# Split start-up constants, a warmed array, clearing in pieces and single last tiles in a two-layer mixture-of-experts block on one Trainium2 core

## The chip, the cores and the metric

The kernel runs on one core of one Trainium2 chip. The metric is the device time in microseconds (us) of one execution. A second number, the span, is what the hardware profiler records from the first to the last instruction of one execution. Engines are named as in the profile: PE (matrix engine, with PEld for its weight loads), DVE (vector), ACT (scalar), POOL (GpSimd), SP (sync, which here only issues transfers). A "q" behind a name is that engine's instruction sequencer, which also issues transfers.

## The reference, cut to what matters

```
x: 8 x 512 tokens of 128 values
x = x + 0.5 * moe(layernorm(x))
x = x + attention(layernorm(x))        # 16 heads of 8, rotary positions
x = x + 0.5 * moe(layernorm(x))

def moe(x):                            # 4096 tokens, 16 experts, 256 places each
    gate = softmax(x @ Wg); idx = argmax(gate)
    loc  = number of earlier tokens with the same expert
    rows with loc < 256 go to expert idx, place loc
    h = relu(rows @ w1[idx]); y = h @ w2[idx]
    return y * gate[idx]  (0 for tokens with loc >= 256)
```

## The kernel before

**Stages.** Each engine has one program written out by hand; they meet only in semaphores. There are four stages in time. (1) Routing of layer 0: all 4,096 tokens are loaded as four groups of 8 tiles of 128 tokens, and a table is built that says for each expert place which token stands there. (2) The 16 experts of layer 0. (3) Attention over 8 sequences, with the second layer's routing spread over it. (4) The 16 experts of layer 1, which write the output.

**Stage 1.** SP issues the 8 loads of the tokens (`load_x`, two to a group), then four of `w1`. ACT issues six small loads, `routing_constants` (identity matrix, gate weights, counting matrices, two expert numberings, token numbers), all on one semaphore `consts_loaded`. PE and DVE both begin by waiting for all six. PE then averages the gate weights over the features (`average_gate`), turns the groups (`turn_group`, 8 transposes each), multiplies them with the centred gate (`group_logits`), counts (`count_group`) and adds to the table (`add_to_table`). ACT copies each turned group out of PSUM (`keep_group`) and behind each copy issues one 1 MB load of `w2` (`load_w2`); after the fourth it computes its share of the marks (`mark_last_places`, one call for each group), without which `add_to_table` can't go. DVE finds each token's expert (`choose_group`), its place (`place_group`), marks, and at the end reads the table (`read_table`, `token_of`). PE issues its steps in this fixed order, so `count_group` of group 2 stands behind `add_to_table` of group 0.

**Clearing.** A scratch tensor `slots` in DRAM (4,096 rows of 146 values) is filled by layer 1's routing and has to hold "no token" rows before that. ACT clears it with one 2.3 MB transfer behind its last mark, just ahead of the experts (`clear_slots`). POOL waits for it (`slots_cleared`) only after the 16 experts of layer 0.

**Experts.** For expert n of layer 0 POOL issues two indirect transfers (`gather_slots`, L725; 128 token rows each) that bring the 256 rows. DVE measures and centres them (L757, L774), PE turns them (`turn_slots`, L834), ACT copies (L870), PE multiplies with `w1` (L842), ACT rectifies (L874), PE multiplies with `w2` (L862: two tiles of 128 places, 8 instructions each), and DVE scales or adds (L786 in layer 0, L826 in layer 1). PE's order is: experts n+1 in, expert n out, with the turning of expert n+2 between the two tiles. `w1`, rows and results stand in rings of four, hidden values in rings of two. In layer 1 both output tiles are signalled by one increment, added by two DVE instructions with one increment (`y_used`), and written by two indirect transfers on POOL (`scatter_rows`, L886). POOL also computes a power of each expert's variance (`invert_slot_deviation`, L769), three experts ahead of the scatter:

```
for n in range(first, last):
    if n + 3 < last:
        invert_slot_deviation(pool, n + 3, (n + 3) % UNROLL)
    scatter_rows(pool, n)
```

ACT's exponentials of expert 31 (`slot_exponentials`) need that power.

**Filling.** `keep_array_busy(count, bank)` issues constant bf16 matmuls of 256 columns (L348); 48 stand between the table and the experts of layer 0.

## Time and profile before

| | |
|---|---|
| time, median of 3 runs | 613.0 us (612.53 to 613.96) |
| the profiled execution: its own time | 612.57 us |
| its span | 610.5 us |
| busy: PE, DVE, ACT, POOL | 561.8, 439.5, 374.0, 395.9 us |
| stage 1, to the end of `token_of` | 0 to 32.7 us |
| layer 0's experts, first turning to last output tile | 42.8 to 108.1 us |
| attention | to about 518 us |
| layer 1's experts, first turning to last scatter | 536.5 to 601.9 us |

The span is 2.1 us shorter than the execution's own time. Engine programs run side by side, so the busy sums say little about one stage; a stage is read from which instruction starts late in it, and from what that one waited for. In a row of the timeline, the text in brackets is the idle time ahead of the instruction and what ended it; "issue" there means that the profile shows no other engine or transfer as the releaser.

### The profile page before, as it was taken

How to read it: one execution, taken by the hardware profiler on the slowest of the kernel's cores; microseconds unless marked ns; L12 is line 12 of the kernel's file. 1: busy time of each engine (PE TensorE's matmuls, PEld its weight loads, DVE VectorE, ACT ScalarE, POOL GpSimd, SP SyncE). 2: the span in 40 equal slices, each digit the busy share in tenths (PEclk: the TensorE clock that was granted, in tenths of full speed). 3: DMA queues.
4: the chain of work that ended last, by engine and by line, in shares of the span. 5: the costliest groups of instructions: out<-in, count | busy, mean ns of one | idle time of the engine just before them, and what ended most of it. 6: DMA issues, size and time to landing. Idle time of an engine off the chain costs nothing.

```text
span 610.5 us, 13303 instructions
## 1 busy us (share of the span) xinstructions
PE 561.8 (92%) x4980; PEld 302.1 (49%) x4980; DVE 439.5 (72%) x938; ACT 374.0 (61%) x518; POOL 395.9 (65%) x630
## 2 busy tenths in 40 slices
PE   4779999998899999999999999999999998999991
PEld 4659889874322333333333323333333333889991
DVE  5834553478988888888988988988899960256651
ACT  2614343012578888887887887887887887045550
POOL 1165688639768776888888888866733514237773
PEclk9779999999999999999999999999999999999996
DMA  9853652143411251261161162152151201135530
GB/s 254 240 192 101 203 170 72 36 144 100 132 61 63 68 177 55 65 193 61 46 207 67 41 206 71 47 186 69 48 181 41 62 19 32 32 91 148 141 86 23
DMA packets 59025, 64.59 MB, mean 106 GB/s; under 512 B 8438, under 2 KB 41999, under 8 KB 58962
## 3 DMA queue, kind: packets, MB, share of 16 engines
q1 hardware_dynamic: 49897, 47.82, 25.5%
q0 software_dynamic: 4096, 8.18, 4.6%
q10 hardware_dynamic: 4969, 7.75, 4.2%
q8 instruction: 40, 0.66, 0.5%
q14 instruction: 23, 0.19, 0.1%
HBM read 37.04 MB, written 23.66 MB: 99 GB/s over the span
## 4 chain that ended last, share of the span: by engine, by line
PE 67%; POOL 12%; issue 10%; ACT 4%; DVE 2%; DMA 2%; ACTq 0%; POOLq 0%; DVEq 0%
PE psum L1520 20%; PE psum L1497 11%; PE psum L1429 9%; PE psum L862 7%; PE psum L842 6%; ACT probs L1506 3%; POOL slot_rows L725 3%; POOL prep_xn L1251 2%; PE psum L348 2%; PE psum L1293 2%; POOL prep_y L1097 1%; PE psum L675 1%; PE psum L423 1%; POOL prep_rstd L1243 1%; PE psum L1535 1%
## 5 line engine op out<-in xcount | busy, mean ns | idle before, releaser
L1441 DVE TENSOR_REDUCE neg_max<-psum 128x2 f32<-128x1024 f32 x256 | 304.2, 1220 | 37.3 <-PE psum L1429 33.8
L1506 ACT ACTIVATE probs<-psum 128x1024 f32<-128x1024 f32 x256 | 260.9, 1024 | 57.0 <-PE psum L1497 47.3
L1520 PE MATMUL psum<-probs,v_ring 128*32 128x256 f32 x2048 | 163.4, 391 | 1.8 <-ACT probs L1506 1.8
L1429 PE MATMUL psum<-k_ring,q_ring 48*128 48x512 bf16 x512 | 98.3, 382 | 4.0 <-DVE neg_max L1441 1.3
L1497 PE MATMUL psum<-q_ring,k_ring 51*128 51x512 bf16 x512 | 99.8, 386 | 2.2 <-DVE neg_max L1441 1.8
L1497 PEld LDWEIGHTS psum<-q_ring,k_ring 51*128 51x128 bf16 x512 | 24.5, 92 | 108.0 <-issue 62.3
L1520 PEld LDWEIGHTS psum<-probs,v_ring 128*32 128x32 f32 x2048 | 40.4, 108 | 65.3 <-issue 49.8
L862 PE MATMUL psum<-w_sb,hidden 128*128 128x128 f32 x512 | 66.6, 275 | 0.0
L874 ACT ACTIVATE hidden<-psum 128x512 f32<-128x512 f32 x64 | 38.2, 597 | 45.4 <-PE psum L842 45.4
L862 PEld LDWEIGHTS psum<-w_sb,hidden 128*128 128x128 f32 x512 | 64.1, 192 | 1.5
L842 PE MATMUL psum<-slot_xn_t,w_ring 128*128 128x256 f32 x256 | 62.4, 387 | 0.9 <-ACT slot_xn_t L870 0.9
L348 PE MATMUL psum<-counters 128*128 128x256 bf16 x458 | 55.5, 280 | 0.0
L842 PEld LDWEIGHTS psum<-slot_xn_t,w_ring 128*128 128x128 f32 x256 | 47.1, 194 | 6.9 <-ACT slot_xn_t L870 1.7
L348 PEld LDWEIGHTS psum<-counters 128*128 128x128 bf16 x458 | 44.9, 100 | 8.9 <-issue 2.6
L1429 PEld LDWEIGHTS psum<-k_ring,q_ring 48*128 48x128 bf16 x512 | 25.4, 93 | 44.5 <-ACT probs L1506 24.2
L702 POOL DMA_INDIRECT slots<-stage,dest x32 | 32.0, 1001 | 18.0 <-DVE dest L663 9.9
L725 POOL DMA_INDIRECT slot_rows<-x,token_of x32 | 33.2, 1038 | 13.1 <-issue 7.6
L769 POOL TENSOR_TENSOR slot_rstd<-slot_spread,minus_half 128x2 f32<-128x2 f32 x32 | 23.0, 719 | 27.4 <-DVE slot_spread L777 21.8
L870 ACT COPY slot_xn_t<-psum 128x256 f32<-128x256 f32 x32 | 11.9, 373 | 44.9 <-PE psum L834 44.9
L1097 POOL DMA_INDIRECT prep_y<-y_rows,y_row_of x32 | 33.5, 1047 | 8.7 <-issue 7.6
L886 POOL DMA_INDIRECT out<-new_rows x32 | 32.1, 1002 | 9.1 <-issue 7.0
L1326 POOL TENSOR_TENSOR proj<-proj,rope_sb 128x512 f32<-128x512 f32 x28 | 35.3, 1285 | 3.9 <-DMA proj<-proj 3.8
(184 smaller groups left out, 613.5 us busy)
## 6 DMA issues: line engine op xcount, KB each, us to landing
w_ring<-w SPq DMA_DIRECT2D x32, 256.0 KB, 2.9
q_ring<-qk_rows SPq DMA_DIRECT2D x64, 96.0 KB
k_ring<-qk_rows SPq DMA_DIRECT2D x62, 96.0 KB
qk_rows<-parts SPq DMA_DIRECT2D x15, 384.0 KB, 3.5
qk_rows<-parts SPq DMA_DIRECT2D x15, 256.0 KB, 3.6
proj<-proj SPq DMA_DIRECT2D x48, 64.0 KB, 1.9
slots<-stage ACTq DMA_DIRECT2D x1, 2336.0 KB, 9.8
slot_rows<-slots SPq DMA_DIRECT2D x16, 146.0 KB, 2.4
```

Source lines behind the costliest of these rows:

```text
L348: nc.tensor.matmul(psum[:, bank, 0:2 * P], counters[:, 0, :], counters[:, :, :].rearrange("p a b -> p (a b)"), start=True, stop=True)
L725: pool.indirect_dma_start(out=slot_rows[:, k, s, 0:D], out_offset=None, in_=x[:, :], in_offset=bass.IndirectOffsetOnAxis(ap=token_of[:, s, ...
L842: i = nc.tensor.matmul(psum[:, 2 + 2 * (k % 2) + c // 2, (c % 2) * CAP:(c % 2 + 1) * CAP], w1_ring[:, k, c * P:(c + 1) * P], slot_xn_t[:, ...
L862: i = nc.tensor.matmul(psum[:, 6 + k % 2, s * D:(s + 1) * D], hidden[:, k % 2, c, s * P:(s + 1) * P], w2_sb[:, e, c, :], start=c == 0, sto ...
L874: nc.scalar.activation(hidden[:, k % 2, c:c + 2, :], psum[:, 2 + 2 * (k % 2) + c // 2, :].rearrange("p (c n) -> p c n", c=2), ACT.Relu).th ...
L1097: pool.indirect_dma_start(out=prep_y[:, n % 2, t, :], out_offset=None, in_=y_rows[:, :], in_offset=bass.IndirectOffsetOnAxis(ap=y_row_of[: ...
L1326: unit.tensor_tensor(proj[:, 2 * c + side, :], proj[:, 2 * c + side, :], rope_sb[:, side, :], ALU.mult).then_inc(rope_step, 1)
L1429: i = nc.tensor.matmul(psum[:, ring_bank(("max", q, j)) + par, :], q_ring[rows, g, pair, tile * P:(tile + 1) * P], k_ring[rows, g, pair, : ...
L1441: nc.vector.tensor_reduce(neg_max[:, q % 2, :, j], psum[:, bank:bank + 2, :], AX.X, ALU.max, negate=True).then_inc(max_used, 1)
L1497: i = nc.tensor.matmul(psum[:, ring_bank(("scores", q, j)) + par, :], k_ring[rows, g, pair, tile * P:(tile + 1) * P], q_ring[rows, g, pair ...
L1506: nc.scalar.activation(probs[:, tile, 2 * pair:2 * pair + 2, :], psum[:, bank:bank + 2, :], ACT.Exp, scale=SCALE).then_inc(scores_used, 1)
L1520: i = nc.tensor.matmul(psum[32 * head:32 * head + 32, BENCH["weighed", pair], columns], v_ring[:, q % QUADS, tile, head, :], probs[:, tile ...
```

## The change

Six edits:

1. Identity matrix and gate weights get a semaphore of their own, `gate_loaded`; the other four constants stay on `consts_loaded`, which PE now waits for only ahead of the first `count_group`. DVE centres the gate first and then measures group 0, and waits for the rest afterwards. The issue order of the six loads on ACT stays.
2. `warm_array`: PE issues 20 constant f32 matmuls of 128 columns (two instructions each) once a matrix of constants is set, and 4 more behind `average_gate`.
3. `clear_slots` is cut in four pieces of 584 KB, issued by ACT behind experts 8 to 11 of layer 0 (the first with the small write of the "no row").
4. 34 instead of 48 constant matmuls behind the table.
5. Experts 30 and 31: each output tile has its own signal, add and scatter, and the second tile goes to another PSUM bank.
6. In layer 1 POOL computes the power of expert 31 behind the scatter of expert 28, not ahead of it; in `add_expert` the copy of the row numbers goes ahead of the waits.

```diff
+        def warm_array(pe, count):
+            for _ in range(count):
+                nc.tensor.matmul(psum[:, 6, 0:P], averaging[:, :], averaging[:, :], start=True, stop=True)
...
         def add_expert(dve, n):
-            dve.wait_ge(weight_step, 4 * (n - EXPERTS) + 4)
-            dve.wait_ge(y_placed, n + 1)
             wait_rows(dve, n)
             nc.vector.tensor_copy(new_rows[:, k, :, D].bitcast(I32), slot_rows[:, k, :, D].bitcast(I32))
+            dve.wait_ge(weight_step, 4 * (n - EXPERTS) + 4)
             for s in range(ST):
+                dve.wait_ge(y_placed, tiles_done(n, s))
                 i = nc.vector.scalar_tensor_tensor(new_rows[:, k, s, 0:D], out_place(n, s),
...
-            i.then_inc(y_used, 1)
+                if n >= FINELY or s == ST - 1:
+                    i.then_inc(y_used, 1)
...
+        FINELY = 2 * EXPERTS - 2
+        def tiles_done(n, s):
+            return n + 1 if n < FINELY else FINELY + ST * (n - FINELY) + s + 1
...
         def scatter_rows(pool, n):
-            pool.wait_ge(y_used, n + 1)
             for s in range(ST):
+                pool.wait_ge(y_used, tiles_done(n, s))
                 pool.indirect_dma_start(
...
-                if n + 3 < last:
+                if n + 3 < last - 1:
                     invert_slot_deviation(pool, n + 3, (n + 3) % UNROLL)
                 scatter_rows(pool, n)
+                if n + 3 == last - 1:
+                    invert_slot_deviation(pool, n + 3, (n + 3) % UNROLL)
...
+        CLEAR_BEHIND = (8, 9, 10, 11)
...
+                if layer == 0 and n in CLEAR_BEHIND:
+                    clear_slots(act, CLEAR_BEHIND.index(n))
...
-            pool.wait_ge(slots_cleared, 16)
+            pool.wait_ge(slots_cleared, 16 * len(CLEAR_BEHIND))
...
-            dve.wait_ge(consts_loaded, 16 * len(routing_constants))
-            dve.wait_ge(carried_clear, 1)
+            dve.wait_ge(gate_loaded, 16 * len(gate_constants))
+            centre_gate(dve)
+            for piece in range(3):
+                measure_piece(dve, 0, piece)
+            dve.wait_ge(consts_loaded, 16 * len(routing_constants))
+            dve.wait_ge(averaging_and_carry_set, 2)
             dve.wait_ge(iotas_ready, 2)
             steps = Steps(dve, group_step)
-            for piece in range(3):
-                measure_piece(dve, 0, piece)
-            centre_gate(dve)
...
-            clear_slots(act)
             act_experts(act, 0)
...
-            pe.wait_ge(consts_loaded, 16 * len(routing_constants))
-
+            pe.wait_ge(averaging_and_carry_set, 1)
+            warm_array(pe, 20)
+            pe.wait_ge(gate_loaded, 16 * len(gate_constants))
             average_gate(pe)
+            warm_array(pe, 4)
             turn_group(pe, 0)
             turn_group(pe, 1)
             pe.wait_ge(wg_ready, 1)
             group_logits(pe, 0)
             group_logits(pe, 1)
             turn_group(pe, 2)
+            pe.wait_ge(consts_loaded, 16 * len(routing_constants))
             count_group(pe, 0)
...
-            keep_array_busy(pe, 48, 0)
+            keep_array_busy(pe, 34, 0)
```

## Rows read from the trace of the kernel before

**Rows 1.** Timeline, PE, start of stage 1: start us, us, engine, line, operation, count

```profile
8.41 0.61 PE L354 MATMUL psum<-wg_sb,averaging 128*128 128x16 f32 x2 [8.41 <-DMA numbers<-token_number]
8.86 3.65 PE L405 MATMUL psum<-ident,probs 128*128 128x128 f32 x16
...
16.30 1.04 PE L405 MATMUL psum<-ident,probs 128*128 128x128 f32 x8
```

**Rows 2.** Timeline, ACT: issue of the fourth `w2` load, and its first mark

```profile
18.87 3.74 ACTq L1842 DMA_DIRECT2D w_sb<-w  x1
...
22.74 1.30 ACT L500 ACTIVATE probs<-place_iota,all_loc 128x256 bf16<-128x256 bf16 x3 [2.95 <-issue]
```

**Rows 3.** Windows: busy us of each engine, then PEclk, DMA share, GB/s

```profile
20.00:23.00 3.00, 2.94 (x26) 2.77 (x25) 2.84 (x14) 0.26 (x1) 0.00 (x0) 1.00 1.05 296
```

**Rows 4.** Chain of waits, 20 to 33.6 us: start us, us, what

```profile
22.95 2.17 issue
...
32.50 0.20 DVE token_of L587
```

**Rows 5.** DMA queues, first 36 to 37, then 38 to 39 us: packets, MB, share

```profile
q10 hardware_dynamic: 164, 0.38, 103.4%
...
q0 software_dynamic: 52, 0.13, 37.5%
```

**Rows 6.** Issue to landing: the clearing, the gather issued at 35.23, all 32 gathers

```profile
slots<-stage ACTq DMA_DIRECT2D x1, 2336.0 KB, 9.8
...
slot_rows<-x,token_of POOLq DMA_INDIRECT x1, 6.1
...
DMA to landing us min/median/max: 2.6/3.1/6.1
```

**Rows 7.** Timeline, start of layer 0's experts

```profile
35.23 0.99 POOL L725 DMA_INDIRECT slot_rows<-x,token_of  x1 [0.31 <-issue]
...
42.80 0.44 PE L834 MATMUL psum<-ident,slot_xn 128*128 128x128 f32 x2 [2.85 <-DVE slot_xn L774]
...
49.16 1.05 PE L862 MATMUL psum<-w_sb,hidden 128*128 128x128 f32 x8
```

**Rows 8.** Timeline, start of layer 1's experts

```profile
538.37 0.38 PE L834 MATMUL psum<-ident,slot_xn 128*128 128x128 f32 x2
...
541.31 1.05 PE L862 MATMUL psum<-w_sb,hidden 128*128 128x128 f32 x8
```

**Rows 9.** Timeline row of the constant matmuls; windows with PEclk as third number from the end

```profile
32.08 7.88 PE L348 MATMUL psum<-counters 128*128 128x256 bf16 x48
...
40.00:44.00 4.00, 0.73 (x3) 0.50 (x4) 2.49 (x15) 0.37 (x1) 3.09 (x4) 1.00 0.21 56
44.00:47.00 3.00, 3.00 (x9) 2.32 (x8) 1.97 (x13) 0.86 (x2) 2.79 (x5) 0.50 0.08 22
...
69.00:70.00 1.00, 0.00 (x0) 0.00 (x0) 0.93 (x6) 0.00 (x0) 0.00 (x0) 1.00 0.97 304
```

**Rows 10.** Timeline, measuring of experts 7 and 12, and PE's turning of 12

```profile
68.97 0.49 DVE L757 BATCH_NORM_STATS2 slot_stats<-slot_rows 128x6 f32<-128x128 f32 x2 [2.20 <-DMA slot_rows<-x,token_of]
...
88.66 0.49 DVE L757 BATCH_NORM_STATS2 slot_stats<-slot_rows 128x6 f32<-128x128 f32 x2 [0.51 <-DMA slot_rows<-x,token_of]
...
90.08 0.38 PE L834 MATMUL psum<-ident,slot_xn 128*128 128x128 f32 x2
```

**Rows 11.** Timeline, POOL and DVE at the end of layer 1

```profile
588.92 0.98 POOL L886 DMA_INDIRECT out<-new_rows  x1 [0.30 <-issue]
...
590.39 0.72 POOL L769 TENSOR_TENSOR slot_rstd<-slot_spread,minus_half 128x2 f32<-128x2 f32 x1 [0.50 <-DVE slot_spread L777]
...
595.67 0.60 DVE L826 SCALAR_TENSOR_TENSOR new_rows<-psum,slot_weight,slot_rows 128x128 f32<-128x128 f32 x2
...
597.07 0.97 POOL L886 DMA_INDIRECT out<-new_rows  x1 [0.89 <-DVE new_rows L826]
...
600.89 0.97 POOL L886 DMA_INDIRECT out<-new_rows  x1 [0.30 <-issue]
```

More of the change, by code:

```diff
@@ L177, in macaron_block_kernel @@
         consts_loaded = sem("consts_loaded")
+        gate_loaded = sem("gate_loaded")
         weights_loaded = sem("weights_loaded")
@@ L185, in macaron_block_kernel @@
         token_iota_ready = sem("token_iota_ready")
-        averaging_ready = sem("averaging_ready")
+        averaging_and_carry_set = sem("averaging_and_carry_set")
         wg_mean_placed = sem("wg_mean_placed")
@@ L200, in macaron_block_kernel @@
         carried = sem("carried")
-        carried_clear = sem("carried_clear")
         group_step = sem("group_step")
@@ L819, in add_expert @@
             k = n % UNROLL
[L820 to L821 removed]
             wait_rows(dve, n)
             nc.vector.tensor_copy(new_rows[:, k, :, D].bitcast(I32), slot_rows[:, k, :, D].bitcast(I32))
+            dve.wait_ge(weight_step, 4 * (n - EXPERTS) + 4)
             for s in range(ST):
[L826 removed]
+                dve.wait_ge(y_placed, tiles_done(n, s))
+                i = nc.vector.scalar_tensor_tensor(new_rows[:, k, s, 0:D], out_place(n, s),
                                                    slot_weight[:, s:s + 1], slot_rows[:, k, s, 0:D],
                                                    ALU.mult, ALU.add)
[L829 removed]
+                if n >= FINELY or s == ST - 1:
+                    i.then_inc(y_used, 1)
         def turn_slots(pe, n, k):
@@ L835, in turn_slots, with out_place @@
             i.then_inc(slot_xn_t_placed, 1)
+        FINELY = 2 * EXPERTS - 2
+        def out_place(n, s):
+            k = n % UNROLL
+            bank = k % 2 if n >= FINELY and s == ST - 1 else 6 + k % 2
+            return psum[:, bank, s * D:(s + 1) * D]
+        def tiles_done(n, s):
+            return n + 1 if n < FINELY else FINELY + ST * (n - FINELY) + s + 1
         def expert_in(pe, n, turned=None):
@@ L861, in expert_out @@
                         turn_slots(pe, n + 2, (k + 2) % UNROLL)
-                    i = nc.tensor.matmul(psum[:, 6 + k % 2, s * D:(s + 1) * D], hidden[:, k % 2, c, s * P:(s + 1) * P],
+                    i = nc.tensor.matmul(out_place(n, s), hidden[:, k % 2, c, s * P:(s + 1) * P],
                                          w2_sb[:, e, c, :], start=c == 0, stop=c == FC - 1)
@@ L865, in expert_out @@
                         i.then_inc(w1_used, 1)
-            i.then_inc(y_placed, 1)
+                if n >= FINELY or s == ST - 1:
+                    i.then_inc(y_placed, 1)
         def keep_slots_turned(act, n, k):
@@ L1824, in macaron_block_kernel @@
         LAST_ROUTED = BATCH - 1
-        routing_constants = [(ident[:, :], identity), (wg_sb[:, :], wg), (counters[:, :, :], count_mats), (iota_e[:, :], expert_iota[0]),
+        gate_constants = [(ident[:, :], identity), (wg_sb[:, :], wg)]
+        routing_constants = [(counters[:, :, :], count_mats), (iota_e[:, :], expert_iota[0]),
                              (iota_low[:, :], expert_iota[1]), (numbers[:, :], token_number)]
@@ L1843, in load_w2, with clear_slots @@
                           ).then_inc(w2_loaded[c], 16)
-        def clear_slots(eng):
-            eng.wait_ge(empty_ready, 4)
-            eng.dma_start(y_rows[TOKENS:TOKENS + 1, :], stage[0:1, 0, 0, 0:D]).then_inc(no_row_written, 16)
-            eng.dma_start(slots.rearrange("(n p t) c -> p n (t c)", p=P, t=TT),
+        def clear_slots(eng, piece):
+            blocks = TOKENS // (P * TT)
+            share = blocks // len(CLEAR_BEHIND)
+            if piece == 0:
+                eng.wait_ge(empty_ready, 4)
+                eng.dma_start(y_rows[TOKENS:TOKENS + 1, :], stage[0:1, 0, 0, 0:D]).then_inc(no_row_written, 16)
+            eng.dma_start(slots.rearrange("(n p t) c -> p n (t c)", p=P, t=TT)[:, piece * share:(piece + 1) * share, :],
                           stage[:, 0, :, :].rearrange("p t c -> p (t c)").unsqueeze(1)
-                          .broadcast_to([P, TOKENS // (P * TT), TT * ROW])).then_inc(slots_cleared, 16)
+                          .broadcast_to([P, share, TT * ROW])).then_inc(slots_cleared, 16)
         @block.sync
@@ L1938, in _ @@
         def _(dve):
-            nc.vector.memset(averaging[:, :], 1.0 / P).then_inc(averaging_ready, 1)
-            nc.vector.memset(carry[:, :], 0.0).then_inc(carried_clear, 1)
+            nc.vector.memset(averaging[:, :], 1.0 / P).then_inc(averaging_and_carry_set, 1)
+            nc.vector.memset(carry[:, :], 0.0).then_inc(averaging_and_carry_set, 1)
             nc.vector.memset(k_ring[:, :, :, :], 1.0).then_inc(ring_cleared, 1)
@@ L2012, in _ @@
         def _(act):
+            for dst, src in gate_constants:
+                act.dma_start(dst, src).then_inc(gate_loaded, 16)
             for dst, src in routing_constants:
```

2 lines of the change are left out of this document (removed).

## The prediction, made before the changed kernel had run

> **What bounds the kernel now.** I read the chain of waits first, by stage, then for each place that the change touches the timeline and the DMA queues of the same microseconds. The chain says that the kernel is a string of stages, each of which hands its lateness on: the attention and both expert loops are paced by engines at work, and nothing in them makes up for a late start. So the question at each edit is by how much the next stage starts earlier.
>
> Stage 1: PE starts at 8.41, released by the last of the six constants [rows 1]. Its first 16 transposes take 3.65 us, 218 ns from one to the next, while 8 of the same kind later take 1.04 us, 110 ns from one to the next [rows 1]. The first run at half speed, at 1.2 GHz, though the windows give a granted clock of 1.00 for these microseconds as for all before 23. Further on the chain stands on "issue" from 22.95 for 2.17 us, ahead of the first adding to the table [rows 4]. Nothing is wrong with PE there. ACT's marks are late: ACT issued the fourth w2 load for 3.74 us, until 22.6, and begins to mark at 22.74 [rows 2]. In that time the DMA engines run at a share of 1.05 and 296 GB/s [rows 3]: ACT's sequencer waits for room behind the w2 loads. From there ACT's marks of group 0, count of group 2, placing and marking of 2 and 3 follow one another with little gap until token_of at 32.50 [rows 4].
>
> Layer 0's experts: the second gather, which completes expert 0's rows, is issued at 35.23, lands 6.1 us later, and PE turns them at 42.80 [rows 6, 7]. All gathers together have 2.6 at least and 3.1 in the median [rows 6]. What is different at 35 us is the clearing: 9.8 us from issue to landing for 2,336 KB [rows 6], and the queues show how it stands in the way: from 36 to 37 ACT's queue (q10) fills 103% of the engines, and POOL's queue (q0), which had its first gather issued since 33.66, moves its first packets in the 38 to 39 window [rows 5]. Then PE's clock is at 1.00 from 40 to 44, in which PE is busy for 0.73 us of 4, and at 0.50 from 44 to 47 [rows 9]: the first expert is worked at half speed.
>
> End: POOL's indirect scatters, 1.27 us apart, are what ends last, at 601.86 [rows 11]. What lies behind them in the span (8.6 us) and around it (2.1) is not touched.
>
> **Part by part.**
>
> **A. Constants and warming: 0.2 us.** Gate constants have landed by about 5. PE starts its 40 warming instructions at about 1.0. If all run at the 218 ns of [rows 1] they end at 9.7; if all at 110 ns, at 5.4. Before, the array ran at half speed for the first 4 us of its work and then at full speed. I take 4 to 6 us at half (18 to 27 instructions), the rest at 110 ns: end at 7.4 to 8.4. With average_gate (0.3) and 8 more instructions (0.9) the first turning starts near 9.3 where it was 9.0, but 16 transposes take 1.8 instead of 3.5. Logits then start at 11.4 instead of 12.3: they need only group 0's copy (1.0 us on ACT) and find PE free. Choosing on DVE moves with them, 0.9 earlier (from 0.8 later to 2.1 earlier). The DVE order costs nothing: centring waits for PE's average at about 8.6, measuring takes 2.5 us from there, and logits come later still. But all of this runs into ACT: the fourth w2 load, however early it is issued, is taken in full only when the w2 bytes ahead of it have moved, and the DMA engines are full already [rows 3]. Counting of group 2 stands behind the adding of group 0 on PE, and that behind ACT's first mark [rows 2, 4]. So I pass on 0.2 us, for a w2 stream that starts a little sooner; the ends are 0 and 1.3 (ACT released as early as the rest). Nothing stands on the four later constants: they land at 8.4, counting comes after 15.
>
> The Trainium skill (TensorE: Matmul & The Clock Gate, "The HAM clock gate") has it that the array's default is half rate and that sustained activity releases it. Rows 1 agree with that by durations, and the granted clock of that stretch does not. By the granted clock alone the warming would be 4.4 us of work and would speed nothing up; by the page it turns 3.5 us of transposes into 1.8. Either way ACT hides it.
>
> **B. The clearing leaves the first gathers: 3.3 us.** The second gather is issued at 35.03 and lands 2.8 us later (between least and median of [rows 6]; ends 2.6 and 3.7, the latter a later gather beside other loads), at 37.8 instead of 41.3. PE then turns at 39.3: 1.5 us behind the landing as now (42.80 behind 41.33). With A's 0.2 that is 3.5 earlier.
>
> **C. First expert at full speed: 0.8 us.** Turning of expert 1 needs the fourth gather, two steps of 1.3 us (0.99 and 0.31, [rows 7]) behind the second, so it comes at 41.9. From there layer 1 shows the way at full clock: 2.94 us from turning to output (538.37 to 541.31 [rows 8]). Output starts at 44.8, where it was 49.16 [rows 7]. A, B and C together: 4.3 us. If the clock falls as it does now, I count C as nothing: the 2.94 grow by about what the fourth gather's earlier place gives.
>
> The 34 constant matmuls: 48 took 7.88 us [rows 9]. With 213 ns at half and 111 ns at full speed that is 25 at half and 23 at full. 34 then take 25 x 0.213 + 9 x 0.111 = 6.3 us, 7.2 if all are at half: from 31.9 to 38.2, or 39.1. Both are ahead of the turning at 39.3, so the count costs nothing; 48 would have ended at 39.8 and cost 0.5. The hole that is left is 0.2 to 1.1 us, then half-idle 2 us. A hole of 1.4 us at 69, with PE at work before and after, left the clock at 1.00 [rows 9]; the one in which it fell was 2.8 us and more half-idle time behind it. I take it that it stays.
>
> **D. The four pieces: minus 1.0 us.** On ACT each issue is some 0.4 us (the whole one was 0.40, the small write 0.49) in idle time of 1.4 an expert: nothing. On the DMA engines 584 KB is a quarter of what took about 6.2 us to move, 1.55 us, at a share of 0.5 to 0.6 in which there is room. The cost is again gathers behind a piece. Gather 12 is issued at 83.58 and 84.95, the first piece at about 84.3; expert 12 was measured at 88.66, 0.51 late already, and PE turned it at 90.08, right behind DVE's 1.3 us of measuring and centring, with some 0.1 to spare [rows 10]. So what the piece adds there, PE pays. Gathers 13 and 15 have 0.2 to 0.5 of slack, gather 14 none. That such a thing reaches PE is seen at 68.97, where attention's constants held a gather for 2.20 us [rows 10]. If a gather waits for a whole piece: 4 x 1.55 = 6.2 us, less slack. If it interleaves: 0. I take 1.0: nearly one piece's drain at the first, small sums behind (a late PE gives the next gather time). Range 0 to 3; above that, see below.
>
> The skill (DMA: Bandwidth & Descriptors, "Queues, rings and completion order") has the engines go round between queues at packet granularity. Rows 5 don't agree: a gather's packets waited while q10 drained. By the page D would be near 0; by the rows up to 6.
>
> **E. The end: 0.9 us.** POOL is free of expert 27's scatters at 589.90 and waits 0.5 for DVE, then works 0.72 on the power of expert 31, and starts 28's scatter at 591.31 [rows 11]. In the new order 28's scatters go at 590.2 and 591.5, the power from about 592.7 to 593.4, 29's at 593.6 and 594.9, and 30's first at 596.2. Its tile is placed at 594.5 and added by 594.9, so it is there; now it waits for both tiles' adds (595.67 + 0.60) and starts at 597.07 [rows 11]. Four scatters from 596.2, 1.27 apart, end at 600.98 instead of 601.86: 0.9. Only single tiles without the move would give 0.6. The power of expert 31 comes 2.3 us later to ACT, which then rectifies expert 31 about 0.8 later, until 595.1; PE wants it at 595.4. That is 0.3 of cover. If it is gone, PE's last 1.8 us shift, and POOL, which takes expert 31's tiles from 598.7, has over a microsecond in hand. The added waits between two scatters cost nothing to see: the gap is 0.30 with a wait in it (between experts) and without. Ends for E: 0.6 and 1.1.
>
> **Sum.** 612.57 - 0.2 - 3.3 - 0.8 + 1.0 - 0.9 = 608.4 by the profiled execution. The three runs' median is 0.4 above that execution, so I forecast 608.8.
>
> **Rivals** (each as a median of runs).
> - Clock falls in the first expert all the same: C is gone, 609.6. For it: PE is half idle from 38 to 42. Against: the hole at 69.
> - ACT is released with the rest and the table is 1.3 earlier: 607.7. For it: I can't see the queue's room, only the length of the issue. Against: full DMA engines.
> - Pieces cost 3: 610.8.
> - The change doesn't do what it says: the first gathers are slow for themselves (first use of the path) and not by the clearing. Then B and C are nothing and what is left is E, less D: 612.1 to 613. For it: they are the first ones. Against: the third and fourth take 3.6 and 3.9, and q0 starts as q10 ends [rows 5].
> - Slower: gathers 12 to 15 are each held for a whole piece. 4 x 1.55 = 6.2 against 5.2 gained: 614.0. It decides from 1.3 us a piece. For it: rows 5 and 68.97. Against: a gather can only be held by a piece issued ahead of it, and three of the four have slack or are issued nearly with it.
>
> **Numbers.** Forecast as it stands (own range 607.6 to 610.0): 0.54. Table earlier: 0.12. Clock falls: 0.13. Pieces cost 3: 0.09. Gathers slow for themselves: 0.07. Slower: 0.05. About 0.2% (1.2 us) is what a measurement of this kernel can tell from no change. Faster: 0.90, same: 0.05, slower: 0.05. The range for 8 in 10 is 606.9 to 611.0: A at its upper end with D at nothing below, D at 3 above.
>
> **What would show it.** A: first transposes near 110 ns, ACT's marks still at 22.5 behind a longer fourth issue. B: second gather lands 2.6 to 3.1 after issue; turning near 39.3. C: first output tile at 44.8, granted clock 1.00 from 40 to 47. D: DVE's idle ahead of experts 12 to 15, 1 us more in all. E: scatters of expert 28 ahead of the power, last scatter 0.9 less behind the last PE tile than now. Wrong would make me: turning after 40.5, a clock of 0.50 behind it, or holes of over 1.3 us at each piece.

## The result, and the profile after

The changed kernel takes 609.42 us in the median (607.98 to 613.08, 12 runs); the kernel before, beside it, 612.85 (610.56 to 622.39, 12 runs). The ratio is 0.9947, with a 95% interval of 0.9924 to 0.9969: 3.2 us faster (4.7 to 1.9). The forecast was 608.8. Here and below the medians are over all executions, and a ratio leaves out those more than 1.5% above the fastest of their kernel. The profiled execution took 608.98 us with a span of 606.8, which is 3.7 us less than that of before.

**Start of stage 1.** The timeline of PE after the change, as in [rows 1]: start, us, engine, line, operation, count.

```profile
1.04 6.62 PE L354 MATMUL psum<-averaging 128*128 128x128 f32 x40 [1.04 <-DVE carry L1967]
...
8.62 1.91 PE L409 MATMUL psum<-ident,probs 128*128 128x128 f32 x16
```

The 16 transposes that took 3.65 us now take 1.91: the array runs at full speed behind its warming, as the durations show (the granted clock reads 1.00 before and after). What ACT makes of that is next in its timeline, to be held against [rows 2]:

```profile
17.50 4.69 ACTq L1866 DMA_DIRECT2D w_sb<-w  x1
22.32 1.30 ACT L504 ACTIVATE probs<-place_iota,all_loc 128x256 bf16<-128x256 bf16 x3 [4.18 <-issue]
```

The fourth w2 load is issued 1.37 us earlier and holds ACT 0.95 us longer. The first mark comes 0.42 earlier and no more.

**Start of the experts.** PE and DVE after, against [rows 7]; then the windows, against [rows 9] (busy us of PE, PEld, DVE, ACT, POOL; granted clock; DMA share; GB/s):

```profile
31.66 5.86 PE L348 MATMUL psum<-counters 128*128 128x256 bf16 x34
38.71 0.44 PE L838 MATMUL psum<-ident,slot_xn 128*128 128x128 f32 x2 [1.20 <-DVE slot_xn L778]
...
44.14 1.05 PE L878 MATMUL psum<-w_sb,hidden 128*128 128x128 f32 x8
```

```profile
37.37 0.49 DVE L761 BATCH_NORM_STATS2 slot_stats<-slot_rows 128x6 f32<-128x128 f32 x2 [4.95 <-DMA slot_rows<-x,token_of]
```

```profile
36.00:40.00 4.00, 2.34 (x18) 1.67 (x17) 1.36 (x8) 0.37 (x1) 2.98 (x4) 1.00 0.19 49
40.00:44.00 4.00, 3.47 (x18) 2.76 (x17) 2.67 (x16) 2.09 (x4) 3.36 (x4) 1.00 0.18 49
44.00:47.00 3.00, 3.00 (x24) 2.88 (x23) 1.22 (x7) 1.04 (x3) 2.78 (x4) 1.00 0.39 112
```

Expert 0's rows are measured at 37.37, and the first output tile starts at 44.14 where it was 49.16. The clock holds at 1.00 where it fell to 0.50.

**The pieces.** DVE's measuring of experts 10, 12 and 13, and what reaches PE, against [rows 10]:

```profile
75.67 0.49 DVE L761 BATCH_NORM_STATS2 slot_stats<-slot_rows 128x6 f32<-128x128 f32 x2 [1.12 <-DMA slot_rows<-x,token_of]
...
84.24 0.49 DVE L761 BATCH_NORM_STATS2 slot_stats<-slot_rows 128x6 f32<-128x128 f32 x2 [1.59 <-DMA slot_rows<-x,token_of]
88.67 0.49 DVE L761 BATCH_NORM_STATS2 slot_stats<-slot_rows 128x6 f32<-128x128 f32 x2 [1.24 <-DMA slot_rows<-x,token_of]
```

```profile
77.06 0.44 PE L838 MATMUL psum<-ident,slot_xn 128*128 128x128 f32 x2 [0.42 <-DVE slot_xn L778]
...
85.59 0.44 PE L838 MATMUL psum<-ident,slot_xn 128*128 128x128 f32 x2 [0.84 <-DVE slot_xn L778]
90.02 0.44 PE L838 MATMUL psum<-ident,slot_xn 128*128 128x128 f32 x2 [0.48 <-DVE slot_xn L778]
```

PE waits twice behind the first two pieces, 0.84 and 0.48. (The gathers of experts 12 and 13 are issued at 78.08 to 82.79, the pieces at 78.07 and 81.28.) The wait at 77.06 belongs to none. The third and fourth piece, issued at 86.07 and 90.50, bring DVE no wait. The DMA queues from 79 to 80, in packets, MB and share of the engines, have one row:

```profile
q10 hardware_dynamic: 166, 0.39, 103.4%
```

That is ACT's queue with the first piece. The gather issued at 78.08 moves no packet in this microsecond, and lands 4.79 after its issue.

**The end.** POOL's timeline, against [rows 11]:

```profile
589.61 0.74 POOL L773 TENSOR_TENSOR slot_rstd<-slot_spread,minus_half 128x2 f32<-128x2 f32 x1
590.72 1.04 POOL L903 DMA_INDIRECT out<-new_rows  x1 [0.36 <-issue]
...
593.35 0.97 POOL L903 DMA_INDIRECT out<-new_rows  x1 [0.30 <-DVE new_rows L829]
...
597.17 0.97 POOL L903 DMA_INDIRECT out<-new_rows  x1 [0.30 <-issue]
```

The power now stands ahead of the scatters of expert 29 (590.72). From there each scatter begins 1.27 to 1.34 us behind the one before it, without the wait of 0.89 us that stood ahead of expert 30's in [rows 11]. From PE's last w2 row (590.76; before 593.56) to the start of the last scatter it is 6.41 us, where it was 7.33.

**Attention** was expected to move rigidly. From the first maximum DVE takes in attention to PE's first turning of layer 1 it took 398.56 us after and 397.10 before: 1.46 of the gain went there. Set side by side, ACT's instructions in attention are 0.34 us later than before at 251 us of after and 1.60 later at 280 (both counted from that first maximum), so most of it was lost between. The windows of after show what stood there:

```profile
268.00:270.00 2.00, 1.39 (x14) 0.45 (x14) 1.09 (x2) 0.96 (x1) 1.68 (x3) 1.00 0.38 113
270.00:272.00 2.00, 1.99 (x20) 1.35 (x18) 1.97 (x4) 1.09 (x2) 2.00 (x2) 0.82 0.42 126
272.00:274.00 2.00, 2.00 (x20) 0.34 (x12) 0.55 (x2) 1.32 (x2) 1.78 (x6) 0.50 0.16 61
274.00:276.00 2.00, 2.00 (x23) 0.48 (x15) 1.61 (x2) 1.20 (x3) 1.86 (x3) 0.83 0.00 0
```

Its PE timeline names the hole (idle time of PE) ahead of it:

```profile
268.61 0.39 PE L1520 MATMUL psum<-q_ring,k_ring 51*128 51x512 bf16 x2 [0.91 <-DMA q_ring<-shift_t]
```

PE waited 0.91 us for a transfer that the change does not touch, and the clock was at 0.50 from 272 on. No 2 us window of before's attention is below 0.97.

### The profile page after: what moved, and what is told of

It reads as the page before. It is cut to its first block and busy times, and to the rows that moved or that the text cites. A ratio compares the mean times of both kernels' runs of the same rounds, so it can differ in the third digit from the quotient of the medians.

```text
span 606.8 us, 13375 instructions
## 1 busy us (share of the span) xinstructions
PE 565.2 (93%) x5014; PEld 304.5 (50%) x5014; DVE 439.9 (72%) x938; ACT 374.0 (62%) x518; POOL 395.7 (65%) x630
## 5 line engine op out<-in xcount | busy, mean ns | idle before, releaser
L858 PE MATMUL psum<-slot_xn_t,w_ring 128*128 128x256 f32 x256 | 60.9, 381 | 0.9 <-ACT slot_xn_t L887 0.9
L348 PE MATMUL psum<-counters 128*128 128x256 bf16 x444 | 53.5, 279 | 0.0
L348 PEld LDWEIGHTS psum<-counters 128*128 128x128 bf16 x444 | 43.4, 100 | 8.4 <-issue 2.6
```

The lines of the kernel that those rows point to most:

```text
L348: nc.tensor.matmul(psum[:, bank, 0:2 * P], counters[:, 0, :], counters[:, :, :].rearrange("p a b -> p (a b)"), start=True, stop=True)
L858: i = nc.tensor.matmul(psum[:, 2 + 2 * (k % 2) + c // 2, (c % 2) * CAP:(c % 2 + 1) * CAP], w1_ring[:, k, c * P:(c + 1) * P], slot_xn_t[:, ...
```

## The experiments

Twelve experiments, in four groups of 4, 4, 3 and 1, with 12 executions each unless a number is given; each group has its own runs of the kernel before (median 614.22, 614.44, 613.92 and 613.81 us), so ratios are what compares. All ratios are to the kernel before, and all kernels but the pieces alone are the changed one with the edit shown. "Turning" is PE's first of expert 0, "output" the first w2 tile, "hole" PE's idle time ahead of the turning; "attention" as above.

**The clearing put back ahead of the experts.**

```diff
+            clear_slots(act)              # whole, 2.3 MB
             act_experts(act, 0)
...
-                if layer == 0 and n in CLEAR_BEHIND:
-                    clear_slots(act, CLEAR_BEHIND.index(n))
```

> The changed kernel with one thing undone: the clearing is again one 2.3 MB transfer, issued by ACT behind its last mark and ahead of the experts. My theory (the clearing holds the first gathers): the second gather lands near 41 instead of 37.4, expert 0 is turned near 42.4 instead of 38.7, and with only 34 constant matmuls PE's hole is 5 us; the clock falls and the first output tile comes near 48.7 instead of 44.1. Experts 12 to 15 lose no time to pieces (1.0 us back). In all 3 to 4 us slower than the changed kernel: near 612.5, equal to the kernel before but for 0.4 at the front and 0.9 at the end. Rival (first gathers are slow for themselves): landing and turning as in the changed kernel, and 1 us faster than it.

Measured: 613.71 us, ratio 0.9979 (0.9944 to 1.0014). The first two gathers land 4.8 to 5.7 us after their issue, where the changed kernel has 2.5 to 2.7. DVE's row, with its wait:

```profile
39.54 0.49 DVE L761 BATCH_NORM_STATS2 slot_stats<-slot_rows 128x6 f32<-128x128 f32 x2 [7.20 <-DMA slot_rows<-x,token_of]
```

The turning comes at 41.01, behind a hole of 3.35 us; the clock is at 0.50 from 44 to 46 and the output starts at 47.37, 3.2 us later than with the pieces. From there to the last w2 row of the layer it is 55.17 us, against 55.21 before and 56.24 with pieces. So the clearing's place is worth 3.2 at the first output, and 1.07 goes back to the pieces: 2.16 at the last w2 row of the layer. Two numbers missed what was expected. The second gather lands at 39.5 and not near 41, as the clearing took 7.8 us here and 9.8 before. And the median is 4.3 us above that of the changed kernel (another group), where the rows of the experts give 2.2: this profile's attention took 399.79 us, with the clock at 0.50 at 170.

**The front undone.**

```diff
-            warm_array(pe, 20)
             pe.wait_ge(gate_loaded, 16 * len(gate_constants))
+            pe.wait_ge(consts_loaded, 16 * len(routing_constants))
             average_gate(pe)
-            warm_array(pe, 4)
...
-            pe.wait_ge(consts_loaded, 16 * len(routing_constants))
             count_group(pe, 0)
```

and DVE measures group 0 ahead of centring the gate, behind all constants.

> The changed kernel without its front: no warming matmuls, PE and DVE wait for all six constants, DVE measures before it centres. My theory (ACT's issue of the fourth w2 load sets the table's time): logits 1.5 us later, but the first mark of ACT only 0.4 later (22.7) and token_of at 32.5 instead of 32.1; 0.4 slower than the changed kernel. Rival (the front's gain goes through): token_of 1.5 later, 1.5 slower.

Measured: 610.45 us, 0.9940 (0.9907 to 0.9972). ACT's first mark is at 23.64 and the last step of the table at 33.15, 1.06 later than in the changed kernel. But this front is also that of before and of the next experiment but one, whose marks come at 22.74 and 21.82. A single profile can't price this part. The mean over the three executions with the old front is 32.33 for the table's last step; over the eight with the new one (and w2 as it was), 32.09. That is 0.24 us, but the three lie between 31.34 and 33.15 and the eight between 31.81 and 32.44, so the size of this part is not shown.

**The end undone.**

```diff
-        FINELY = 2 * EXPERTS - 2
+        FINELY = 2 * EXPERTS
...
-                if n + 3 < last - 1:
+                if n + 3 < last:
                     invert_slot_deviation(pool, n + 3, (n + 3) % UNROLL)
                 scatter_rows(pool, n)
-                if n + 3 == last - 1:
-                    invert_slot_deviation(pool, n + 3, (n + 3) % UNROLL)
```

> The changed kernel without single last tiles and with the power of expert 31 ahead of the scatter of expert 28. My theory (POOL's scatters set the end): PE's last tile at the same time, last scatter 0.9 later, 0.9 slower than the changed kernel. Rival (the end is set by PE or by the landing alone): no difference.

Measured: 611.07 us, 0.9951 (0.9916 to 0.9985). From PE's last w2 row to the last scatter 7.29 us, against 6.41. Its profiled span (605.8) is shorter than the changed kernel's all the same, since its attention took 396.45. Its windows at the place of after's fall:

```profile
268.00:270.00 2.00, 2.00 (x19) 0.80 (x17) 1.80 (x3) 1.61 (x2) 1.68 (x3) 1.00 0.33 105
270.00:272.00 2.00, 2.00 (x23) 1.08 (x26) 1.48 (x4) 1.05 (x3) 2.00 (x2) 1.00 0.40 133
272.00:274.00 2.00, 1.80 (x21) 0.45 (x13) 1.74 (x2) 1.96 (x3) 1.77 (x6) 1.00 0.12 44
```

The same stage with the same instructions, a wait of 0.19 us for the same transfer, and no fall.

**The pieces alone:** the kernel before, with only the clearing moved behind experts 8 to 11 (so 48 constant matmuls, old front, old end).

> The kernel before with the third edit alone: four pieces behind experts 8 to 11, still 48 constant matmuls. My theory: second gather lands near 37.9, but PE ends its 48 matmuls at 39.9 and turns right behind, the first output tile comes near 44.7, granted clock 1.00; experts 12 to 15 lose 1 us; 3.3 to 3.7 faster than the kernel before, nearly all of the change. Rival (the gain is the sum of many parts): 1 to 2 faster.

Measured: 610.83 us, 0.9946 (0.9914 to 0.9978). This one edit has as large a measured gain as the six. Turning at 38.58, right behind the 48 matmuls, output at 43.52, 5.64 earlier than before. Of that, 1.16 is the table, whose last step came at 31.34 with the same front as before (32.50): the scatter of that stage, not the edit. The other 4.48 are the rows that come early and the clock, which stays at 1.00 in the first expert.

**The clearing whole, behind the marks of group 1.**

```diff
             for g in range(GROUPS):
                 mark_last_places(act, g)
+                if g == 1:
+                    clear_slots(act)      # whole
```

> The changed kernel with the whole clearing as one transfer issued by ACT behind its second mark, at about 26, when the w2 loads end (27.3) and before the first gather's packets (35). Theory (only overlap with gathers costs): it moves from 27.5 to 33.7, first gathers land as in the changed kernel (37.4), first output tile at 44.1, and experts 12 to 15 get back the 1.0 us that the pieces cost; 1.0 faster than the changed kernel at the end of layer 0's experts. Rival (a big transfer delays gathers for longer than its own length, or delays ACT's third mark): turning after 39.5, no gain or a loss.

Measured: 609.34 us, 0.9914 (0.9884 to 0.9944). The rows come as early as with pieces (37.52) and behind 75 us DVE waits for no expert's rows longer than 0.89 us (1.59 with pieces), but the clock fell in the first expert. Its PE timeline and windows:

```profile
38.86 0.44 PE L838 MATMUL psum<-ident,slot_xn 128*128 128x128 f32 x2 [2.08 <-DVE slot_xn L778]
...
45.72 0.50 PE L878 MATMUL psum<-w_sb,hidden 128*128 128x128 f32 x3
```

```profile
40.00:42.00 2.00, 1.48 (x7) 1.02 (x7) 1.29 (x7) 0.60 (x1) 1.58 (x2) 0.74 0.22 59
42.00:44.00 2.00, 2.00 (x6) 1.58 (x6) 1.25 (x7) 0.53 (x2) 1.67 (x3) 0.50 0.14 39
```

It fell once more from 68 to 72, behind a wait of 2.11 us for rows that attention's constants held up. So this profile doesn't show the gain that the median has, and the interval of its ratio overlaps that of the changed kernel (0.9924 to 0.9969): that an early clearing beats the pieces is not shown by these runs.

**The fourth w2 load behind ACT's first mark.**

```diff
                 keep_group(act, g)
-                load_w2(act, g)
+                if g < 3:
+                    load_w2(act, g)
...
                 mark_last_places(act, g)
+                if g == 0:
+                    load_w2(act, 3)
```

> The changed kernel with the fourth w2 load issued behind ACT's first mark instead of ahead of it. Theory (the issue of that load holds ACT, which holds the table): ACT marks group 0 near 19 instead of 22.3, token_of 1.3 to 1.6 earlier (30.6), turning of expert 0 near 37.2, 1.3 to 1.6 faster at the first output tile. Rival (ACT is held by something else, or the wait moves to the next mark): token_of less than 0.5 earlier.

Measured: 608.01 us (10 runs), 0.9903 (0.9873 to 0.9933). ACT's timeline, to be held against the two rows of after above:

```profile
19.00 1.30 ACT L504 ACTIVATE probs<-place_iota,all_loc 128x256 bf16<-128x256 bf16 x3
20.34 0.93 ACT L508 ACTIVATE probs<-probs,v_ring 128x768 bf16<-128x768 bf16 x1
20.40 2.31 ACTq L1866 DMA_DIRECT2D w_sb<-w  x1
22.75 1.30 ACT L504 ACTIVATE probs<-place_iota,all_loc 128x256 bf16<-128x256 bf16 x3 [1.48 <-issue]
```

The mark is 3.32 us earlier, the table's last step 1.66 earlier (30.43), the output 1.58 earlier (42.56). So the issue of a load held ACT and the table, as the prediction argued. The load was moved only with the new front. How much of the 1.66 needs the warmed array, and how much the old front would have given too, was not run: in the kernel before, ACT's fourth copy ended at 19.79, 2.95 us ahead of its first mark.

**Both together:** the two diffs above in one kernel.

> Both: fourth w2 load behind the first mark, whole clearing behind the second. Theory: the gains add up as long as the clearing has ended when the gathers' packets come. The w2 bytes end at 27.3, the clearing at 33.7, the gathers' packets come at 33.5: just free. 2.3 to 2.6 faster than the changed kernel at the end of layer 0's experts. Rival: the first gather is held for the last piece of the clearing, and only 1.5 is left.

Measured: 607.59 us (6 runs), 0.9897 (0.985 to 0.9944). Output at 42.57, and from there 54.77 us to the layer's last w2 row, against 56.24 with pieces. The first gather landed 3.85 us after its issue, 1.1 later than in the changed kernel, but the second, which completes the rows, after 2.71.

**48 constant matmuls in place of 34** (`keep_array_busy(pe, 48, 0)`).

> The changed kernel with 48 constant matmuls behind the table as before. They would end near 39.1 where expert 0 is ready at 38.7. By my prediction 0.4 late at the first turning. But the turning of expert 1 waits for the fourth gather (41.3), and PE's four matmuls between have 0.5 us of room: so the first output tile at 44.1 as now, and no difference in time. Rival: 0.4 slower throughout.

Measured: 615.73 us, 0.9954 (0.9916 to 0.9992). The start is as expected: turning at 39.15, output at 44.13. The times are not: 8 of 12 lie above 612 us. (Four of them, from 617.4 to 620.3, are more than 1.5% above the fastest, so the ratio says little of them.) In the profiled execution (span 614.0) attention took 403.63 us. Its windows and PE's row there:

```profile
360.00:362.00 2.00, 1.99 (x24) 0.60 (x22) 1.94 (x3) 1.65 (x3) 1.97 (x2) 1.00 0.47 135
362.00:364.00 2.00, 0.28 (x8) 0.00 (x0) 1.00 (x1) 0.56 (x1) 1.52 (x3) 1.00 0.59 165
364.00:366.00 2.00, 1.36 (x8) 0.41 (x12) 0.22 (x1) 0.71 (x1) 1.99 (x3) 0.51 0.50 177
366.00:372.00 6.00, 6.00 (x40) 2.45 (x32) 3.19 (x5) 2.78 (x4) 5.55 (x11) 0.50 0.07 25
```

```profile
364.64 0.61 PE L1520 MATMUL psum<-q_ring,k_ring 51*128 51x512 bf16 x2 [2.36 <-DMA q_ring<-shift_t]
```

The same wait as in after, 2.36 us long, and then about 10 us at half the clock. What was to test a filler showed what the runs scatter by, and the last four experiments went to that.

**The changed kernel again.**

> The changed kernel once more, unedited, beside the two others of this call. The question is where the attention stage lost 1.5 us in its profiled execution (398.56 us from the first maximum of attention to the first turning of layer 1, against 397.10 in the kernel before and 396.45 with the end undone, though the instructions are the same). Theory 1: nothing of the change lies in attention; the loss is one fall of the granted clock behind a hole of 0.9 us at 268.6 (the clock is 0.50 from 272 to 274), and such falls come and go from one execution to the next. Then this profile has its falls in another place or none, attention takes 396.4 to 397.2 us where there is none, about 1.5 more for each short one and 4 to 5 more for a long one, the times of all runs fall as their mean granted clock rises, by 0.4 to 0.5 us for each 0.001, and the median is 609 to 611 with a ratio of 0.993 to 0.996. Theory 2: the change shifts the attention against its transfers so that the hole is there each time. Then the clock is again at 0.50 between 270 and 276 and attention takes 398.5 again.

Measured: 609.60 us (607.48 to 615.46, 12 runs), 0.9960 (0.9929 to 0.9991). Attention 397.31, no window of it below 0.97. But this time the clock fell in the first expert, as its PE timeline and windows show:

```profile
31.38 5.33 PE L348 MATMUL psum<-counters 128*128 128x256 bf16 x34
38.50 0.44 PE L838 MATMUL psum<-ident,slot_xn 128*128 128x128 f32 x2 [1.78 <-DVE slot_xn L778]
```

```profile
40.00:42.00 2.00, 1.49 (x7) 1.00 (x6) 0.99 (x6) 0.97 (x2) 1.70 (x2) 0.81 0.27 66
42.00:44.00 2.00, 2.00 (x7) 1.55 (x6) 1.62 (x9) 0.60 (x1) 1.67 (x3) 0.50 0.11 33
44.00:46.00 2.00, 2.00 (x11) 1.78 (x10) 0.50 (x3) 0.81 (x2) 1.82 (x4) 0.84 0.14 33
```

Output at 45.59 behind a turning at 38.50: 7.09 us, where after's profile has 5.43. Theory 1 holds in the main: the fall of after's attention did not come again. In the two sets of 12 runs of this kernel the time falls by 0.43 and 0.61 us for each 0.001 of mean granted clock (correlations -0.85 and -0.97).

**48 again.**

> The changed kernel with 48 constant matmuls in place of 34, once more. In its first run the start was as expected (first output tile at 44.13) but the times fell in two groups, 608.2 to 609.6 and 613.6 to 620.3, and the profiled execution had the clock at 0.50 from 366 to 372. Theory 1: the count costs nothing or 0.4 us, and the two groups are executions with and without falls of the clock in attention, by chance. Then its median here is within 1.5 us of the changed kernel's beside it, with the same slope of time against granted clock. Theory 2: the count itself moves something that makes the clock fall more often. Then its mean granted clock is again about 0.974, against 0.979 for the changed kernel, and it is 3 us or more slower than that.

Measured: 614.24 us, 0.9991 (0.9959 to 1.0023), 4.6 us above the changed kernel beside it; mean granted clock 0.973 in the median, against 0.980. 9 of 12 times lie above 612; its profile is of one of the other three (span 608.0, attention 398.70). Theory 2 as written: the loss came again in the medians. The ratios, 0.9991 and 0.9960, have intervals that overlap, and at the same mean granted clock (0.978, by a straight line of time against clock through each set) it is 1.1 us above the changed kernel: most of the 4.6 goes with the clock.

**Both together again.**

> The changed kernel with the fourth w2 load behind ACT's first mark and the clearing as one transfer behind the second group's marks, once more; only six runs of it are known. Theory 1: both parts of the gain are real. The table is 1.6 us earlier, the experts of layer 0 lose nothing to pieces (1.0), so it is 2.0 to 2.6 us faster than the changed kernel beside it, ratio to the kernel before 0.989 to 0.992. Theory 2: the 1.8 us by which it was faster were the scatter of the attention's clock. Then it is within 0.7 us of the changed kernel at the same mean granted clock.

Measured: 607.67 us (7 runs), 0.9905 (0.9877 to 0.9933), 1.9 us under the changed kernel beside it. Its profile is of its longest run (span 612.7): attention took 405.75 us with the clock at 0.50 to 0.69 from 164 to 172 and 0.50 from 368 to 376. At the same mean granted clock, as above, the gap shrinks to 0.6. So the runs don't separate the two theories: 1.6 us at the table is seen in the rows of three profiles (table's last step 30.43, 30.47, 30.64), and how much of it the time keeps is open between 0.6 and 1.9.

**41 constant matmuls.**

> The changed kernel with 41 constant matmuls in place of 34. In two calls 48 of them were 4.6 to 6 us slower in the median than 34 (614.2 and 615.7 against 609.6 and 609.4) with a mean granted clock of 0.973 and 0.974 against 0.980, though PE turned expert 0 only 0.4 to 0.5 us later. 17 of 24 times lay above 612 with 48 and 7 of 24 with 34. 41 end at about 38.3, ahead of the turning at 38.6, so that nothing is moved by them, and the hole in front of the turning is 0.3 instead of 1.2 to 1.8 us. Theory 1: what hurts with 48 is the shift of everything behind the start, in which PE and the rows meet their holes in attention at other places; then 41 is as fast as 34, 608.5 to 610.5, ratio 0.992 to 0.996, and its first expert always has the clock at 1.00. Theory 2: the number of matmuls itself makes the clock fall more often later on; then 41 lies between, 611 to 613, ratio 0.996 to 1.000, and its mean granted clock near 0.976.

Measured: 610.95 us (11 runs), 0.9952 (0.9921 to 0.9984), mean granted clock 0.976, 3 of 11 above 612; hole 0.84, clock at 1.00 in the first expert, output at 44.20, attention 395.68. The time lies between the two theories' ranges and tells nothing apart.

**The hole and the clock, over the profiles with 34 matmuls, and before:**

| kernel | filler, us | hole, us | clock in the first expert | turning to output |
|---|---|---|---|---|
| both, again | 6.21 | 0.96 | 1.00 | 5.32 |
| front undone | 5.98 | 1.11 | 1.00 | 5.53 |
| both | 6.11 | 1.11 | 1.00 | 5.30 |
| changed | 5.86 | 1.20 | 1.00 | 5.43 |
| w2 behind the mark | 5.85 | 1.23 | 1.00 | 5.48 |
| end undone | 5.85 | 1.24 | 1.00 | 5.49 |
| changed, again | 5.33 | 1.78 | 0.50 | 7.09 |
| clearing early | 5.03 | 2.08 | 0.50 | 6.86 |
| clearing ahead | 6.08 | 3.35 | 0.50 | 6.36 |
| before (48) | 7.88 | 2.85 | 0.50 | 6.36 |

In the three other profiles with 48 matmuls and early rows and in the one with 41 the hole is 0.00 to 0.84 us and the clock stays at 1.00.

Two later places help to judge the table. The hole at 69 of [rows 9] is in all 14 profiles (before, after and the twelve experiments), behind the same gather (expert 7's). It is 1.09 to 1.82 us long in eleven, and the clock stays at 1.00. In the other three it is 2.11 (clearing early), 2.38 (48) and 2.60 us (front undone), and the clock falls, as in the last of them:

```profile
66.00:68.00 2.00, 0.34 (x2) 0.34 (x3) 1.61 (x13) 0.00 (x0) 0.23 (x1) 0.95 0.73 245
68.00:70.00 2.00, 2.00 (x11) 2.00 (x10) 0.40 (x5) 0.37 (x1) 1.56 (x2) 0.50 0.03 11
```

In attention it is less clear. Where after's profile has the hole of 0.91, that of the w2 load behind the mark has one of 0.90, and no fall behind it:

```profile
267.76 0.39 PE L1520 MATMUL psum<-q_ring,k_ring 51*128 51x512 bf16 x2 [0.90 <-DMA q_ring<-shift_t]
```

```profile
272.00:274.00 2.00, 1.80 (x23) 0.54 (x17) 1.74 (x2) 1.86 (x3) 1.87 (x3) 1.00 0.06 24
```

And every profile has a hole of 1.28 to 1.30 us between 163 and 172, behind which the clock fell in three of 14 (clearing ahead, both, both again). The hole of 1.78 us in the table has a fall, where 1.82 at the later place (the changed kernel again) has none. So longer holes have the falls more often, but the length of a hole alone does not say whether the clock falls.

## Why the prediction was right, and where it was not

**The sum.** It gave 608.4 for an execution like the one of before and 608.8 for the median; the profiled execution took 608.98 and the median is 609.42. The sign, the mechanisms and the size of nearly every term held. That the total came so near is in part luck: by the rows the terms brought 0.7 us more than forecast, and attention, where none was forecast to go, took 1.5 back. (The range for 8 in 10 does not quite follow from its terms: 608.8 with 1.1 more from A and nothing for D is 606.7, not 606.9.)

**A, 0.2.** The mechanism is shown, the size is not. The transposes went from 3.65 to 1.91 us and the table's last step came 0.41 earlier in this profile (0.24 in the mean of executions, less than they scatter by). That ACT's issue of the fourth w2 load is what holds it was argued from [rows 2]; moving the load freed 1.66, a little more than the upper end of 1.3. The rival "table 1.3 earlier" needed another edit.

**B, 3.3.** 3.6: rows measured 4.0 earlier, less 0.41 of A. The second gather landed 2.54 us after its issue at 34.81, against 2.8 assumed. The rival by which the first gathers are slow for themselves is out: the same gathers take up to 5.7 us with the clearing ahead of them and 2.7 without. How the queue held them is as in [rows 5]. The Trainium skill (DMA: Bandwidth & Descriptors, "Queues, rings and completion order") has each engine go round between its queues a packet at a time. Taken alone, that would have let the gathers in beside the clearing; in the runs they landed 2.3 to 3.6 us later behind it. The rows show that they wait, and not why.

**C, 0.8.** 0.93 in this profile: turning 4.09 earlier, output 5.02. But it is not there in each execution. In two of the eight profiles with 34 matmuls and early rows the clock fell (changed kernel again, clearing early) and turning to output took 1.4 to 1.7 more. Against before, C was then -0.7 and -0.5, and not nothing as the prediction counted it. The rival "clock falls" was given 0.13; two in eight is more. The step that was thin is the count of the filler: at 6.3 us it would leave a hole of 1.1. It took 5.03 to 6.21 us: the window from 30 to 36 has a granted clock of 0.65 with the clearing early, 0.52 in the changed kernel. A clock that rises early makes the filler end early, and that lengthens the hole behind it. Both falls stand behind the two shortest fillers. That the hole made the clock fall is read from these rows, and not forced by an experiment. The prediction rested it on the hole at 69 that left the clock at 1.00; that was one execution, and in three of the 14 profiles the hole there was longer and the clock fell. The Trainium skill (TensorE: Matmul & The Clock Gate, "HAM oscillation — how this bites in real kernels") tells of waits for a transfer between stretches of work that send the array back to half rate, so that the next stretch begins there. The table agrees in kind (holes of 2.08 and 2.85 us in which PE waits for rows, then 0.50). The case that the Trainium skill tells of has longer waits, a fall in every round and little work between them; a fall behind 0.91 us in an attention that is nearly always busy is not its case.

**The filler.** "Costs nothing" for 34 was right (ended 37.52, turning 38.71). The 0.5 us of 48 was right for the turning in one of its profiles: 1.79 us behind the measuring of the rows, where 34 have 1.34. In the other the rows themselves were 0.56 later and the turning followed them by 1.34. At the first output the first profile had lost nothing (44.13 against 44.14). For the whole kernel it was wrong, by the medians: 4.6 us more than 34 beside it, and 6 in the first pair, which are of different groups. 17 of 24 executions lie above 612, against 7 of 24 with 34. It is not the count as such: the pieces alone have 48 too, at a mean clock of 0.982, and none of its 12 runs is under 0.980. Why the clock falls more often behind 48 in the changed kernel stays open; 41 did not decide it.

**D, 1.0.** 1.03 in after (5.02 earlier at the first output, 3.99 at the last w2 row), 1.07 against the clearing put back. Gathers behind the first two pieces landed in 4.8 to 5.9 us, the same gathers before in 2.6 to 3.7: they are held 1.1 to 3.3 us, 2.1 in the mean, where a piece's 1.55 was assumed. PE waits 0.84 and 0.48 for it, and its rounds of these two experts (3.73 us undisturbed) take 4.79 and 4.43. That is 1.76 in all; the 1.03 is what is left after other waits of this stage became 0.7 shorter than before, so the size is in part luck. The other two pieces cost nothing at PE, though gather 14 was said to have no slack. The rival that was slower had each hold about right, and was wrong in letting all four reach PE.

**E, 0.9.** 0.92, and 0.88 by undoing it. Both are of the rows; the times of the runs don't separate it.

**What failed: "nothing in them makes up for a late start".** It was read as: the attention moves as a block. It does not. Between the layer's last w2 row and the first maximum 0.26 us more was gained; then attention took 1.46 more time. The terms sum to 4.2 by the prediction and to 5.02 - 1.03 + 0.92 = 4.9 by the rows; with 0.26 gained and 1.46 lost the span has 3.7. Most of the loss (1.26) lies around a clock fall behind a wait for `q_ring<-shift_t`; that such a wait alone does not bring it is seen in the rows under the table. Over the profiles without such a fall attention takes 395.7 to 398.7 us, over those with one 398.6 to 405.8. So even the theory's 396.4 to 397.2 was too narrow. These falls go together with the scatter of the runs. About 0.2% was taken as what a measurement can tell; runs of one kernel spread by 0.7 to 2.1%, and an interval was 0.45% to 0.9% wide. The single edit's 0.9946 and the six edits' 0.9947 can't be told apart; what C and E are worth is known from the rows alone, and what A is worth not even from them.

## What to carry to other kernels

A large transfer without a deadline should not be issued ahead of a small one that an engine waits for: here it cost 3 us at the first output, and where it goes instead is chosen by whose gathers have slack. Look at what an engine's own issue of a load holds up behind it: moving one `dma_start` behind the first mark gave 1.6 us at the table, where warming the array alone had passed on 0.4 or less. Before trusting gains of half a per cent, set each run's time against its mean granted clock. A filler of a fixed count ends sooner when the clock rises early in it (34 took 5.0 to 6.2 us), so judge its hole by the shortest case.

## What was not expected of the hardware

- A wait of 0.91 us ahead of one matmul pair in attention stood 2 to 3 us ahead of a fall of the granted clock to 0.50, and one of 2.36 us ahead of 10 us at 0.50, though PE had been busy for most of the time around; one of 0.90 at the same place of another profile, and eleven of 1.09 to 1.82 at the place of [rows 9], left the clock at 1.00.
- The fourth 1 MB load held ACT's sequencer for 4.69 us when issued at 17.50, and for 2.31 when issued at 20.40 behind the mark: it came free at 22.2 and 22.7.
- Time and mean granted clock go together over the runs of 16 of 17 sets (the four of the kernel before included), at 0.27 to 0.80 us for each 0.001. The one without is the pieces alone, none of whose runs had a mean clock under 0.980.
